# Six experts' down projections with the weights held still, in two rounded parts, and their sum over the experts on GpSimd

## The reference, cut to what matters

```
probs = softmax(xf @ w_router); top 2 of 8, normalised -> cw (token, expert)
h1 = einsum('td,edh->eth', xf, w1); h3 = einsum('td,edh->eth', xf, w3)
y  = einsum('eth,ehd->etd', silu(h1) * h3, w2)         # 8 experts, hidden 256
out = einsum('etd,te->td', y, cw) + silu(xf @ sw1) * (xf @ sw3) @ sw2
x = x + out
```

## Time and profile before

| | |
|---|---|
| runs shown | 1046.45, 1043.82, 1048.62 us, median 1046.45 |
| profiled execution | 1046.03 us, of which the trace's span is 1044.3 |
| busy over the span | PE 903.1 us (86%), DVE 811.1 (78%), ACT 544.6 (52%), POOL 420.2 (40%) |
| PE busy, L1356 in all layers | 247.3 us, 960 matmuls |
| PE busy, L1349 of `ew` (this layer's down projections) | 70.2 us, 576 matmuls |

### The profile page before, as it was taken

The page is one execution under the profiler, slowest core; times in us unless marked ns, Lnnn a source line. Parts: engine busy times, 40 slices in busy tenths (PEclk is TensorE's granted clock), DMA queues, the critical chain, the costliest instruction groups (busy, mean ns, idle before and its releaser), DMA issues.

```text
span 1044.3 us, 15167 instructions
## 1 busy us (share of the span) xinstructions
PE 903.1 (86%) x5628; PEld 665.5 (64%) x5628; DVE 811.1 (78%) x1450; ACT 544.6 (52%) x979; POOL 420.2 (40%) x400
## 2 busy tenths in 40 slices
PE   6967877778899999989885767899968999999997
PEld 4432222223688888866654546576646789999997
DVE  6799999999767555573897886599975588878886
ACT  6456566654653222236533223466645467677775
POOL 6479999999200101112982354544420001011110
PEclk9979999999999999999987997599999999999999
DMA  6000000000001001000000001000000000000001
GB/s 186 1 0 1 0 1 0 0 1 1 1 2 31 16 16 31 16 1 1 1 0 1 1 1 41 1 2 2 2 1 1 1 21 21 6 16 21 21 21 41
DMA packets 19860, 13.82 MB, mean 13 GB/s; under 512 B 3067, under 2 KB 18313, under 8 KB 19786
## 3 DMA queue, kind: packets, MB, share of 16 engines
q1 hardware_dynamic: 19786, 12.84, 4.4%
HBM read 11.79 MB, written 1.05 MB: 12 GB/s over the span
## 4 chain that ended last, share of the span: by engine, by line
PE 52%; DVE 17%; ACT 5%; issue 3%; POOL 1%; DVEq 0%; ACTq 0%; POOLq 0%
PE ps L1356 19%; PE ps L1349 17%; PE ps L1569 3%; DVE small L1233 2%; PE ps L1743 2%; DVE G L1236 2%; PE ps L1685 1%; PE ps L1639 1%; PE ps L1400 1%; DVE R L1194 1%; DVE stats L812 1%; DVE ps L1199 1%; PE ps L1675 1%; DVE ps L1183 1%; DVE R L1185 1%
## 5 line engine op out<-in xcount | busy, mean ns | idle before, releaser
L1356 PE MATMUL ps<-xhl,whl 128*128 128x512 f32 x960 | 247.3, 407 | 12.7 <-DVE xhl L834 5.1
L1356 PEld LDWEIGHTS ps<-xhl,whl 128*128 128x128 f32 x960 | 179.1, 194 | 52.3 <-issue 13.4
L784 ACT ACTIVATE G<-ps,w_exp_bi 128x512 f32<-128x512 f32 x128 | 89.9, 702 | 65.9 <-PE ps L1356 54.9
L1349 PEld LDWEIGHTS ps<-R,G 128*128 128x128 f32 x1024 | 119.0, 192 | 6.4 <-DVE G L1279 4.1
L1349 PE MATMUL ps<-R,G 128*128 128x128 f32 x1024 | 119.7, 275 | 3.1 <-DVE G L1279 3.1
L356 POOL TENSOR_TENSOR R<-G,R 128x1024 f32<-128x1024 f32 x43 | 100.5, 2352 | 19.4 <-ACT R L550 15.8
L942 DVE TENSOR_TENSOR_SCAN R<-ps,R 128x1024 f32<-128x1024 f32 x43 | 97.6, 2279 | 5.7 <-POOL R L365 5.7
L785 ACT ACTIVATE G<-ps,ebs 128x512 f32<-128x512 f32 x144 | 102.0, 708 | 0.0
L649 ACT ACTIVATE G<-ps 128x512 f32<-128x512 f32 x72 | 42.8, 597 | 112.8 <-PE ps L1356 112.8
L1039 DVE SCALAR_TENSOR_TENSOR X<-ps,cw,X 128x128 f32<-128x128 f32 x272 | 76.5, 344 | 23.4 <-PE ps L1349 23.2
L1279 DVE SCALAR_TENSOR_TENSOR G<-G 128x1024 f32<-128x1024 f32 x72 | 91.6, 1272 | 2.5
(11 more groups left out here) (270 smaller groups left out, 1726.2 us busy)
## 6 DMA issues: line engine op xcount, KB each, us to landing
ew<-in_w_dram SPq DMA_DIRECT2D x24, 128.0 KB, 2.2
R<-in_exp_wi_dram SPq DMA_DIRECT2D x8, 256.0 KB, 2.7
R<-in_exp_wo_dram SPq DMA_DIRECT2D x8, 256.0 KB, 3.2
X<-in_x_dram SPq DMA_DIRECT2D x4, 256.0 KB, 3.9
out_dram<-X SPq DMA_DIRECT2D x4, 256.0 KB, 2.3
w_ctxT<-in_ctxT_dram SPq DMA_DIRECT2D x1, 487.5 KB
ew<-in_sw_dram SPq DMA_DIRECT2D x3, 128.0 KB, 2.5
w_W_in<-in_W_in_dram SPq DMA_DIRECT2D x1, 256.0 KB, 3.0
```

What stands on the lines that cost most here:

```text
L784: sc.activation(G[:, 0, slot, m * GT:(m + 1) * GT], banks[:, m, :], ACT.Exp, bias=exp_bias[m])
L1349: ins = mm(bank(o)[:, 0, b * width:(b + 1) * width], lhs(k, b), rhs(k), start=k == 0, stop=k == ks - 1)
L1356: ins = mm(mix(out) if n == N_WIN1 else out, whl[:, wslot(n), i, m * P:(m + 1) * P], rhs, start=k == 0, stop=k == 2)
```

## The change

For experts 2 to 7 (items 8 to 31, `by_feature`) the down projection is turned round: `w2` is the held operand, in two rounded parts (`w2hl`), and the hidden values are streamed, also in two parts (`hl`), 512 tokens at a time (`down_T`). That is two halves of the hidden dimension by three matmuls, and the result has features on partitions, tokens along the row. So the router's weights are needed along the row too and alike on all partitions: TensorE transposes them once in step 7, ScalarE copies the result out, SyncE writes it to DRAM (64 KB) and reads each of the six experts' rows back with a broadcast over 128 partitions (1 MB each) into `cwb`, two slots. The upper part of the hidden values is a ScalarE copy (`hidden_upper`), the lower a VectorE subtraction (`hidden_lower`). GpSimd splits `w2` (`split_w2`). VectorE multiplies the projection with `cwb` (`weigh_out`; for expert 2 into the sum `YT`, after that into one of two slots `yt_new`), GpSimd adds the slot to `YT` (`add_out_T`, items 12 to 31). In steps 30 to 33 TensorE transposes one group of `YT` back (`transpose_YT`, banks 6 and 7), and VectorE adds it to `X` one step later (`add_YT`). The shared expert, expert 1 and expert 8 keep the old form. `hl`, `w2hl` and `cwb` lie in memory that was free in this layer. The weights of the routed experts now lie in `router[:, 5]`. In the second attention semaphores were only merged with those of the first (`hq_mm` into `q_mm` and so on), with their counts moved along; no instruction moves there, and that part of the diff is left out.

```diff
@@ sync
@@ -291,6 +302,16 @@
                     expert0(k % 2, s, a["w1"][k - 1], a["w3"][k - 1], a["w2"][k - 1])
+                if k == 2:
+                    sp.wait_ge(S["cw_rows"], 1)
+                    sp.dma_start(cw_dram, cw_rows).then_inc(S["cw_rows"], 16)
+                    sp.wait_ge(S["cw_rows"], 17)
+                if k * NG in by_feature:
+                    if k >= 4:
+                        sp.wait_ge(S["res0"], NG * (k - 1))
+                    sp.dma_start(cwb[:, k % 2, :].rearrange("p (b t) -> p b t", b=B),
+                                 cw_dram.rearrange("(b e) t -> e b t", e=E)[k - 1].partition_broadcast(P))\
+                        .then_inc(S["cw_odd" if k % 2 else "cw_even"], 16)
@@ gpsimd
+            def split_w2(e):
+                if e >= 4:
+                    pool.wait_ge(S["down0"], NG * (e - 1))
+                src, hi, lo = ew0[:, e % 2, 2, :], w2hl[:, e % 2, 0, :], w2hl[:, e % 2, 1, :]
+                step(gp.tensor_copy(hi, src))
+                gp.tensor_tensor(lo, src, hi.bitcast(F32), ALU.subtract).then_inc(S["w2_split"], 1)
+
+            def add_out_T(c):
+                pool.wait_ge(S["res0"], c + 1)
+                if c >= 4 * NG:
+                    pool.wait_ge(S["yt_acc"], c - NG - 3 * NG + 1)
+                gp.tensor_tensor(YT[:, gcols(c % NG)], YT[:, gcols(c % NG)], yt_new[:, c % 2], ALU.add).then_inc(S["yt_acc"], 1)
             for e in range(2, E + 1):
                 split_e0(e)
+                if e * NG in by_feature:
+                    split_w2(e)
+                for c in range(max(3 * NG, e * NG - 6), e * NG - 2):
+                    add_out_T(c)
+            for c in (E * NG - 2, E * NG - 1):
+                add_out_T(c)
@@ scalar
+            def hidden_upper(i):
+                n = i - by_feature[0]
+                if n >= 2:
+                    act.wait_ge(S["down0"], i - 1)
+                for m in range(M0):
+                    act.wait_ge(S["hid0"], M0 * i + m + 1)
+                    sc.copy(hl[:, i % 2, 0, m * GT:(m + 1) * GT], hidr[:, i % 2, m * GT:(m + 1) * GT])\
+                        .then_inc(S["hid_hi"], 1)
             for i in range((E + 1) * NG):
                 silu_up(i)
+                if i in by_feature:
+                    hidden_upper(i)
+                if i == 2 * NG - 1:
+                    act.wait_ge(S["cwt_mm"], 1)
+                    sc.copy(cw_rows, bank(6)[:, 0, 0:T]).then_inc(S["cw_rows"], 1)
@@ vector
             def hidden(i):
-                if i >= 2:
+                if i - 2 in by_feature:
+                    dve.wait_ge(S["hid_lo"], M0 * (i - 1 - by_feature[0]))
+                elif i >= 2:
                     dve.wait_ge(S["down0"], i - 1)
+            def hidden_lower(i):
+                n = i - by_feature[0]
+                for m in range(M0):
+                    dve.wait_ge(S["hid_hi"], M0 * n + m + 1)
+                    v.tensor_tensor(hl[:, i % 2, 1, m * GT:(m + 1) * GT], hidr[:, i % 2, m * GT:(m + 1) * GT],
+                                    hl[:, i % 2, 0, m * GT:(m + 1) * GT].bitcast(F32), ALU.subtract).then_inc(S["hid_lo"], 1)
+
+            def weigh_out(c):
+                e, g = divmod(c, NG)
+                dve.wait_ge(S["down0"], c + 1)
+                dve.wait_ge(S["cw_odd" if e % 2 else "cw_even"], 16 * (e // 2))
+                if c - 2 >= 3 * NG:
+                    dve.wait_ge(S["yt_acc"], c - 2 - 3 * NG + 1)
+                to = YT[:, gcols(g)] if e == 2 else yt_new[:, c % 2]
+                v.tensor_tensor(to, bank(4 + c % 2)[:, 0, :], cwb[:, e % 2, gcols(g)], ALU.mult).then_inc(S["res0"], 1)
+
+            def add_YT(g):
+                dve.wait_ge(S["yt_mm"], g + 1)
+                dve.wait_ge(S["res0"], NG + g + 1)
+                v.tensor_tensor(X[:, gb(g), :], X[:, gb(g), :], bank(6 + g % 2)[:, 0, :].rearrange("p (b d) -> p b d", b=GB),
+                                ALU.add).then_inc(S["yt_res"], 1)
             for i in range((E + 1) * NG + 1):
+                if i - 2 in by_feature:
+                    weigh_out(i - 2)
                 if i < (E + 1) * NG:
                     hidden(i)
-                if 1 <= i != NG + 1:
+                if i in by_feature:
+                    hidden_lower(i)
+                if 1 <= i != NG + 1 and i - 1 not in by_feature:
...
+                if 0 <= i - E * NG + 1 < NG:
+                    add_YT(i - E * NG + 1)
@@ tensor
+            def down_T(c):
+                e, n = c // NG, c - by_feature[0]
+                pe.wait_ge(S["w2_split"], e - 1)
+                pe.wait_ge(S["res0"], c - 1)
+                for k in range(M0):
+                    pe.wait_ge(S["hid_lo"], M0 * n + k + 1)
+                    for p, (i, j) in enumerate(PARTS):
+                        ins = mm(bank(4 + c % 2)[:, 0, :], w2hl[:, e % 2, i, k * D:(k + 1) * D],
+                                 hl[:, c % 2, j, k * GT:(k + 1) * GT], start=k == p == 0, stop=k == M0 - 1 and p == 2)
+                ins.then_inc(S["down0"], 1)
+
+            def transpose_YT(g):
+                pe.wait_ge(S["yt_acc"], (E - 4) * NG + g + 1)
...
+                    ins = nc.tensor.transpose(bank(6 + g % 2)[:, 0, b * D:(b + 1) * D], YT[:, (g * GB + b) * T:(g * GB + b + 1) * T], ident[:])
+                ins.then_inc(S["yt_mm"], 1)
+                if i == 2 * NG - 1:
+                    pe.wait_ge(S["rt_cw"], 1)
+                    nc.tensor.transpose(bank(6)[:, 0, 0:T], router[:, 5].rearrange("p b e -> p (b e)"), ident[:]).then_inc(S["cwt_mm"], 1)
-                if i >= 1:
+                if i - 1 in by_feature:
+                    down_T(i - 1)
+                elif i >= 1:
                     c = i - 1
...
+                if 0 <= i - E * NG + 2 < NG:
+                    transpose_YT(i - E * NG + 2)
```

More of the change, by code:

```diff
@@ L109, in decoder_program @@
         qhl = sb("qhl", [P, HI, N], F32R)
-        sb("over_G1_to_G4", [P, 4, HI, N])
+        hl = sb("hl", [P, 2, 2, M0 * GT], F32R)
+        sb("over_G2", [P, HI, N])
+        sb("over_half_G3", [P, N])
+        w2hl = sb("w2hl", [P, 2, 2, M0 * D], F32R)
+        sb("over_G3_and_G4", [P, N - 2 * GT + HI * N])
         kz = sb("kz", [P, 2, 2, HQ * LK], F32R)
@@ L190, in decoder_program @@
         cwT = G[0:E, 5, 1, :].rearrange("p (b t) -> p b t", b=B)
+        by_feature = range(2 * NG, E * NG)
+        cwb = G[:, 0, :, :]
+        yt_new = G[:, 2, 0, 0:2 * GT].rearrange("p (s n) -> p s n", s=2)
+        cw_rows = G[:, 2, 0, 2 * GT:2 * GT + T]
+        YT = G[:, 2, 1, :]
+        cw_dram = nc.dram_tensor("cw_by_token", (P, T), F32).ap()
         xi, z1, lam, vv, nb, ww = (GBUF(i) for i in range(6))
@@ L457, in keys @@
                 if b >= 2:
-                    pool.wait_ge(S["hs_mm"], 2 * (b - 1))
+                    pool.wait_ge(S["sc_mm"], NG + 2 * (b - 1))
                 for i in range(2):
@@ L747, in v1_copy @@
             def v1_copy(g):
-                act.wait_ge(S["hv_mm"], g + 1)
-                sc.copy(v1S[0:LK, gb(g), :], bank(4 + g)[0:LK, 0, :].rearrange("p (b d) -> p b d", b=GB)).then_inc(S["hv_ev"], 1)
+                act.wait_ge(S["v_mm"], NG + g + 1)
+                sc.copy(v1S[0:LK, gb(g), :], bank(4 + g)[0:LK, 0, :].rearrange("p (b d) -> p b d", b=GB)).then_inc(S["v_ev"], 1)
             act.wait_ge(S["gated"], NSPAN + 1)
@@ L1051, in add_gated @@
             def add_gated(i):
+                if i >= E * NG:
+                    dve.wait_ge(S["yt_res"], i - E * NG + 1)
+                elif i >= NG:
+                    dve.wait_ge(S["res0"], i - NG + 1)
                 if i >= NG:
-                    dve.wait_ge(S["res0"], i - NG + 1)
-                add_expert(i, cw0, i // NG - 1 if i >= NG else E, "down0", "res0")
+                    add_expert(i, router[:, 5], i // NG - 1, "down0", "res0")
+                else:
+                    add_expert(i, cw0, E, "down0", "res0")
@@ L1056, in _ @@
             probs = router[:, 1]
             for i in range((E + 1) * NG + 1):
+                if i - 2 in by_feature:
+                    weigh_out(i - 2)
                 if i < (E + 1) * NG:
                     hidden(i)
-                if 1 <= i != NG + 1:
+                if i in by_feature:
+                    hidden_lower(i)
+                if 1 <= i != NG + 1 and i - 1 not in by_feature:
                     if i == NG + 2:
-                        weigh(probs, cw0[:, :, 0:E]).then_inc(S["rt_cw"], 1)
+                        weigh(probs, router[:, 5]).then_inc(S["rt_cw"], 1)
@@ L1516, in router_logits @@
                 ins.then_inc(S["rt_mm"], 1)
+            def down_T(c):
[10 more added lines that the diff above has]
+                pe.wait_ge(S["yt_acc"], (E - 4) * NG + g + 1)
+                if g >= 2:
+                    pe.wait_ge(S["yt_res"], g - 1)
+                for b in range(GB):
+                    ins = nc.tensor.transpose(bank(6 + g % 2)[:, 0, b * D:(b + 1) * D], YT[:, (g * GB + b) * T:(g * GB + b + 1) * T], ident[:])
```

(7 more changed lines are left out.)

34 lines of the change are left out of this document (17 added, 17 removed).

## The result

The changed kernel takes 1055.41 us (median of 20 runs, 1050.06 to 1062.43) against 1048.16 of before (20 runs, 1043.82 to 1052.31). The ratio is **1.0063, with a 95% interval of 1.0046 to 1.0081**: slower by about 6.6 us, where 1045.5 and "no change" were forecast. The profiled execution took 1050.61 us with a span of 1048.7, which is 4.6 and 4.4 more than the profiled one of before; the trace can explain these 4.4, not the rest of the 6.6.

A forecast was written before the change was run, and what follows sets the result against it. TensorE alone was taken to bound the 24 steps; -14.9 (steps) + 7.95 + 0.5 + 2.95 (boundaries) + 2.1 + 0.15 (transposes) + 0.7 (tail) = -0.55 us from 1046.03, so 1045.5 us, 8-in-10 range 1038 to 1051.5.

The forecast's parts named there:

- What a step saves: 24 steps of experts 2 to 7: 3.90 us each instead of 4.52, -14.9 us in all (-14.2 to -16.3).
- The mark I set for being wrong: Even steps, away from expert boundaries: over 4.1 us, with VectorE then the bound, would show the forecast wrong.
- The coefficients: First broadcast of the router's weights: lands at 340.1, weighing 8 due at 340.4, lateness counting from about 341.7; no cost.
- rival C: First broadcast: 512 B pieces at 100 GB/s land at 346.6, 5 us late; sum +4.4, 1050.5 us; chance 0.08.
- B's mechanism: Stalls behind steps 4e-1, e = 5 to 8: TensorE's clock falls to half, about +10, 1056 us; chance 0.10.
- The boundaries: Where experts 5, 6, 7 begin: additions behind GpSimd's splits, turns with VectorE, TensorE stalls; 2.65 each, +7.95 us.
- the 0.25 for late lower parts: Expert boundaries: VectorE's lower parts come just late for the second half of a down projection; 0.25 us each.
- expert 8: Where expert 8 begins: down projection 1.0 late, last additions late for the first transposes of the sum; +2.95 us.
- the transposes: Steps 30 to 33: four groups of four transposes of the sum on TensorE, 0.53 a group, +2.1 us.
- the tail: End of the stage: VectorE gets two more additions of 0.69 in steps 33 and 34; +0.7 us (0 to 1.4).
- VectorE's keeping up in an even step: Even steps: VectorE's five instructions take about 3.6 of 3.90 us, so TensorE sets the step, with little to spare.
- rival A: Expert boundaries: stalls mostly hidden, 1.05 each for three, about 1.7 at expert 8; sum -7.1, 1039 us; chance 0.25.

The follow-up runs named there:

- The first experiment: The kernel before, with the down projections of items 8 to 31 computed twice into the same bank: 1089.97 us, a step 6.31 us.
- Long rows: The changed kernel with the coefficients laid out by expert in DRAM, so each broadcast moves 8 KB rows: 1049.23 us, ratio to before 0.9996.
- the experiments on order and on the operand: Changed kernel, GpSimd's additions 4e-6 and 4e-5 ahead of the splits: 1048.52 us; long-rows kernel, lower parts' second input from PSUM (wrong values): 1042.98 us.
- The kernel with both edits: The changed kernel with GpSimd's additions ahead of the splits and the coefficients in 8 KB rows: 1042.71 us, ratio to before 0.9935.
- the trace with the additions first: The changed kernel with GpSimd's additions of items 4e-6 and 4e-5 ahead of expert e's splits: 1048.52 us, ratio to before 1.0002.

## Why the prediction was wrong

It gave the range up to 1051.5 us; the time is 1055.41, and "slower", to which it gave 0.15, is what came. Three steps failed: the first two made the change look better than it is, the third worse. Of the 9.9 us between 1045.5 and 1055.41, 5.1 lie between the forecast and the profiled execution (1050.61), and these the steps below explain, with 0.9 of chance. The other 4.8 lie between the profiled execution and the median. Of those, 2.1 are in the base: the forecast started from the profiled 1046.03, while the kernel before has a median of 1048.16 over 20 runs. The last 2.7 go with the lower clock.

1. **What a step saves** was mis-sized: 0.44 us and not 0.62, 10.6 us and not 14.9. I split 4.52 us into 2.62 and 1.90 by the starts of the weight loads and priced six matmuls from 2.62. The first experiment gives 2.73 and 1.79, and the forecast by these would have been 4.09. I had even seen that "a part of 2.62 is the change to the other kind of matmul", and corrected in the wrong direction. The mark I set for being wrong, steps over 4.1 us with VectorE as the bound, did not come: TensorE still sets the step.
2. **The coefficients** were costed at nothing: 262 GB/s from a stretch of larger pieces, so landing at 340.1. The weighing got them at 349.57, 14.8 us after their issue, and they cost 6.0 us. That is rival C, to which I gave 0.08, and at a price beyond its 4.9: the gap of 4.56 in step 11 and, behind it, nine matmuls of which some ran at 1.2 GHz. B's mechanism, with 0.10, thus came once, for 1.4 us, behind a gap of 4.56; behind the gaps of 1.3 to 1.8 the nine loads take 1.91, and the clock did not fall. That the measured time lies beside B's 1056 is chance. I also passed over expert 3's weights as "due three steps later": GpSimd got them 15.8 us after their issue, more than three steps, and alone this would have stopped TensorE for some 6 us. Long rows take all of it away.
3. **The boundaries** had the right mechanism and too large a size. Turns, the order on GpSimd, the wait of the weighing, the gap at steps 19, 23 and 27: all stand in the trace, and the experiments on order and on the operand show what each of the two is worth. But 2.65 a boundary came to 1.2 to 1.6. At step 19, with T = 376.15, the product ends at about T + 10.5 (forecast 10.8) and TensorE wants it at T + 8.8 (forecast 8.45), two steps of 4.08 instead of 3.90 later; the 0.25 for late lower parts did not come. So this error follows in part from the first one, and gave back some of it.

Right in kind were expert 8 (2.95, measured 2.1), the transposes, the tail, and VectorE's keeping up in an even step. The router's single transpose cost 0.55 and not 0.15: the down projection behind it starts 0.53 late. The kernel with both edits (1042.71, some 6.8 us by its ratio) wins about what rival A asked for, but not for A's reason: the turns are as long as I read them, and its even steps save less than A's sum takes.

The sum put right: -0.55 + 4.3 (steps) + 6.0 (broadcast) - 3.8 (boundaries) - 1.5 (smaller terms) + 0.9 (the stage began late) = +5.4 at the last down projection, and +4.4 at the end of the span. Without the 0.9, which is chance, the change itself costs some 4.5 at the last down projection.

## What to carry to other kernels

Where two kinds of matmul alternate, take the price of each from a run in which one is doubled or absent, not from the starts of its weight loads: here both were misread by 0.11 us, which made most of the difference between 0.62 and 0.44. Price a transfer by its pieces and not by its bytes alone, lay the source of a broadcast out so that a partition reads one long row, and look at what is queued behind it. (Issuing it earlier was not tested.) An in-order engine that is given work of two paces (splits that wait for weights, additions that others wait for) should do the awaited work first; that reordering and the long rows together turned a kernel 0.6% slower than before into one 0.65% faster.

## What the runs showed of the hardware

- A broadcast of 1 MB from DRAM to 128 partitions took 15.1 us in pieces of 512 B and 5.3 us in rows of 8 KB, about 70 and 200 GB/s. With the short pieces, three loads of 128 KB issued behind it took 11.6 us to land in the median instead of the usual 2.2. The Trainium skill (DMA: Bandwidth & Descriptors, section Specifications) names 512 B as the least transfer for line rate; the trace doesn't agree: here pieces of just that size took three times as long as long rows, and the measurement decides.
- GpSimd and VectorE delayed each other where VectorE had two SBUF inputs: GpSimd's subtraction of 512 columns 1.84 instead of 1.29, its cast of 256 columns 0.87 instead of 0.40, VectorE's pair 2.38 instead of 1.46. With one of VectorE's inputs in PSUM neither was delayed. The delays fit turns of a whole instruction each: ahead of step 19, VectorE's second subtraction, begun at 381.31, ended at 382.92, which is 0.56 behind the end of GpSimd's at 382.36.
- Float32r matmuls of 512 columns with a weight load each follow at 0.227 us (18 in a step of 4.08; twelve in 2.73), not at the 0.218 that the starts of the weight loads gave.
- After 4.56 us without a weight load TensorE came back with the granted clock at 0.70 over 5 us, and after 4.99 us in the trace with the additions first at 0.50 for some 6 us; after 1.76 us and less it stayed at 1.00.
